# One program for ffn0's norm, scores, routing, placement and shared expert, with sixteen gathers issued at its end

## The reference, cut to what matters

```
def _L0_ffn_ref(x, w1s, w2s, w3s, W1, W2, W3, Wg):     # x is already normed
    def geglu(x, w1, w2, w3):
        return gelu(x @ w1) * (x @ w2) @ w3            # 128 -> 512 -> 128
    shared = geglu(xf, w1s, w2s, w3s)                  # every token
    idx = argmax(xf @ Wg, axis=-1)                     # one of 8 experts for a token
    final = sum over e of where(idx == e, geglu(xf, W1[e], W2[e], W3[e]), 0)
    return shared + final
x = x + 0.5 * _L0_ffn_ref(_layernorm(x), ...)
```

## Time and profile before

| | |
|---|---|
| three runs | 2185.0, 2183.94 and 2178.56 us; median 2183.94 |
| profiled execution, its own time | 2175.02 us |
| its span, first to last instruction | 2173.3 us |
| busy share of the span | PE 79%, PEld 65%, VectorE 64%, GpSimd 49%, ScalarE 38% |
| mean granted TensorE clock | 0.866 of full speed |

### The profile page before, as it was taken

One profiled execution on the slowest core, in us unless ns is written; L12 is line 12 of the kernel. 1 busy time (PEld: TensorE's weight loads), 2 busy tenths in 40 slices (PEclk: granted clock), 3 DMA queues, 4 the chain that ended last, 5 costly groups with the idle time before them and its releaser, 6 DMA issues. The chain is left out here.

```text
span 2173.3 us, 36779 instructions
## 1 busy us (share of the span) xinstructions
PE 1706.7 (79%) x11054; PEld 1406.2 (65%) x11054; DVE 1397.8 (64%) x3248; ACT 832.5 (38%) x1822; POOL 1068.3 (49%) x1178
## 2 busy tenths in 40 slices
PE   3889951499999999999976989547885488829883
PEld 3459950178888888888863579546874156628782
DVE  4444546499999999999854445484454544573455
ACT  1222212255555555555522222124552233225551
POOL 2006634267777777777630047436774100137772
PEclk9999965699999999999977999857998667659996
DMA  6001130000000000000022001231112100301114
GB/s 208 1 0 45 43 89 0 0 1 1 1 1 1 1 1 1 1 2 1 1 92 79 0 26 48 90 98 38 53 52 72 39 1 0 97 31 51 52 53 135
DMA packets 60900, 82.08 MB, mean 38 GB/s; under 512 B 24720, under 2 KB 30896, under 8 KB 60720
## 3 DMA queue, kind: packets, MB, share of 16 engines
q1 hardware_dynamic: 46640, 51.01, 7.5%
q0 software_dynamic: 14080, 28.86, 4.8%
HBM read 54.93 MB, written 24.90 MB: 37 GB/s over the span
## 5 line engine op out<-in xcount | busy, mean ns | idle before, releaser
L681 POOL DMA_INDIRECT rows_in<-xn_rows,slot_token x220 | 214.8, 976 | 334.6 <-SPq L676 268.8
L687 POOL DMA_INDIRECT y_rows<-y,slot_row x220 | 230.0, 1045 | 113.5 <-DVE y L814 53.4
L726 PE MATMUL ps<-w,inner_slot 128*128 x1760 | 246.3, 284 | 18.4 <-issue 7.7
L1466 DVE SCALAR_TENSOR_TENSOR cv<-ps,cw,cv 128x1021 f32<-128x1021 f32 (+2 forms) x192 | 245.0, 1276 | 17.3 <-ACT cv L1404 14.8
L714 PE MATMUL ps<-gT,w_slot 128*128 128x128 f32 x1760 | 242.1, 282 | 2.0 <-DVE hb L797 1.1
L726 PEld LDWEIGHTS ps<-w,inner_slot 128*128 128x128 f32 x1760 | 217.2, 194 | 30.8 <-issue 26.0
L714 PEld LDWEIGHTS ps<-gT,w_slot 128*128 128x128 f32 x1760 | 222.3, 198 | 4.5 <-issue 4.5
L1573 POOL TENSOR_TENSOR y<-t,sz 128x256 f32<-128x256 f32 x128 | 94.7, 740 | 181.4 <-DVE t L1510 181.4
L797 DVE TENSOR_TENSOR hb<-ps,b 128x512 f32<-128x512 f32 x142 | 97.6, 687 | 112.8 <-PE ps L714 81.6
L1311 PE MATMUL ps<-xnT,win 128*128 128x512 f32 x256 | 133.0, 645 | 31.8 <-DVE cv L1466 27.2
L252 PE MATMUL ps<-ident,xn 128*128 128x128 f32 x192 | 53.1, 432 | 118.7 <-DVE xn L212 118.7
(11 more groups left out here) (256 smaller groups left out, 4261.3 us busy)
## 6 DMA issues: line engine op xcount, KB each, us to landing
w<-in_L_ffn_W SPq DMA_DIRECT2D x6, 2048.0 KB, 11.3
back<-y_rows SPq DMA_DIRECT2D x48, 256.0 KB, 5.7
xn_rows<-xn SPq DMA_DIRECT2D x32, 256.0 KB, 3.9
rows_in<-xn_rows,slot_token POOLq DMA_INDIRECT x220, 2.6
y_rows<-y,slot_row POOLq DMA_INDIRECT x220, 2.3
out_x<-x SPq DMA_DIRECT2D x8, 256.0 KB, 3.5
win<-in_L_attn_in_w SPq DMA_DIRECT2D x1, 1544.0 KB, 10.4
b<-in_L_ffn_b SPq DMA_DIRECT2D x2, 512.0 KB, 11.2
```

The source lines that it names most:

```text
L681: nc.gpsimd.indirect_dma_start(k.rows_in[:, s % AHEAD, :], None, k.xn_rows[:, :], bass.IndirectOffsetOnAxis(ap=k.slot_token[:, s:s + 1], a ...
L687: nc.gpsimd.indirect_dma_start(kept, bass.IndirectOffsetOnAxis(ap=k.slot_row[:, s:s + 1], axis=0), k.y[:, s % RING, :], None).then_inc(sto ...
L726: ins = nc.tensor.matmul(py[:, s % DOWNS, :], k.inner_slot[:, s % RING, b * P:(b + 1) * P], w_dn[:, ds(e * (FB * D) + b * D, D)], start=(b ...
L1466: inc(V.scalar_tensor_tensor(out, piece[:, 0:SEQ - back], m.cw[:, c, i:i + 1], out, ALU.mult, ALU.add), tap_done if i < 2 else a["conv"])
```

## The change

ffn0's first three blocks become one, a new `shared`, and its program is written out for all 32 units with no loop. The norm of group `g + 1`, its transposes (`TURN`), scores (`SCORE`), the routing chain in five pieces, the counting matmuls (`COUNT`) and the placement (`PLACE`) stand between the units of the shared expert. The placement is done as in ffn1, with ScalarE's `match_lanes` and GpSimd's `match_tiles`. The transposes and the scores have one PSUM buffer each where they had two. The weights' semaphore is split: TensorE waits for the shared expert's three loads at its first unit, and SyncE waits for the rest at the end of the block. `rows_in` has 16 buffers, and GpSimd issues the gathers of slots 0 to 15 in this block, after `place_end`; `experts` begins with slot 16. `slot_expert` is written once. In ffn1's `route` the counting of the marks no longer waits for the Exp and the gates. Here is the core of the diff; `prepare` and `take_back` stay as they are, for the other stages.

```diff
+def match_lanes(k, act, n, slots, top):
+    r = n % 2
+    act.wait_ge(k.matched.sem, k.matched.at(n + 1))
+    act.wait_ge(k.placed.sem, k.placed.at(n - 1))
+    k.nc.scalar.activation(k.oh_slot[:, r, :, 0:slots], k.match[:, r, :, 0:slots], ACT.Copy,
+                           scale=k.lane[:, top - 1:top]).then_inc(k.lanes_put.sem, 1)
 def place_tensor(k, pe, n, slots):
     pe.wait_ge(k.onehot.sem, k.onehot.at(n + 1))
+    pe.wait_ge(k.lanes_put.sem, k.lanes_put.at(n + 1))
+    pe.wait_ge(k.tiles_put.sem, k.tiles_put.at(n + 1))
...
+def shared(k, shared_loads, expert_loads, slots, early):
+    TURN = {0: 1, 1: 2, 2: 3, 3: 4, 4: 5, 6: 6, 8: 7}
+    SCORE = {0: 0, 1: 1, 2: 2, 3: 3, 4: 4, 6: 5, 8: 6, 9: 7}
+    COUNT = 12
+    PLACE = {u: u - 17 for u in range(17, 25)}
...
+            statistics(0)                       # VectorE
+            statistics(1)
+            normalise(0)
+            for g in range(2, 5):
+                statistics(g)
+                normalise(g - 1)
+            for u in range(NU):
+                inner(u)
...
+                if u == 10:
+                    dve.wait_ge(logits_kept.sem, logits_kept.at(NG))
+                    route_choose(k, do, 0, L3)
+                if u == 11:
+                    marked(k, k.by_expert[0]).then_inc(marks.sem, 1)
+                if u == 13:
+                    dve.wait_ge(counted.sem, counted.at(1))
+                    route_ranks(k, do, ps_rank, ps_cnt)
+                if u == 14:
+                    route_bases(k, do)
+                if u == 15:
+                    route_positions(k, do, 1)
+                if 16 <= u < 24:
+                    match_vector(k, dve, u - 16, slots)
+                if u == 24:
+                    route_experts(k, do, slots)
+                if u == 25:
+                    place_end(k, dve, NG, slots, 1)
+                if u % FB == FB - 1 and u > FB:
+                    add(u // FB - 1)
...
+            for n in range(NG):                 # GpSimd, after the eight rstd
+                match_tiles(k, pool, n, slots)
+            pool.wait_ge(stored.sem, stored.at(NG))
+            pool.wait_ge(k.place_own.sem, k.place_own.at(5))
+            for s in range(early):
+                nc.gpsimd.indirect_dma_start(k.rows_in[:, s, :], None, k.xn_rows[:, :],
+                                             bass.IndirectOffsetOnAxis(ap=k.slot_token[:, s:s + 1], axis=0)
+                                             ).then_inc(gathered[s].sem, 16)
...
+            turn(0)                             # TensorE
+            for u in range(NU):
+                up_block(u)
+                if u in TURN:
+                    turn(TURN[u])
+                if u in SCORE:
+                    score(SCORE[u])
...
+                if u in PLACE:
+                    place_tensor(k, pe, PLACE[u], slots)
+                if u % FB == FB - 1 and u > FB:
+                    down_group(u // FB - 1)
+            down_group(NG - 1)
...
+            nc.scalar.activation(k.spare[:, 1:2], k.zero[:, 0:1], ACT.Gelu)   # ScalarE
+            copy(0)
+            for u in range(NU):
+                act.wait_ge(up.sem, up.at(u + 1))
+                act.wait_ge(ready.sem, ready.at(u - 1))
+                nc.scalar.activation(k.gl[:, u % 2, :], h1[:, u % 2, :], ACT.Gelu).then_inc(acted.sem, 1)
+                if u in TURN:
+                    copy(TURN[u])
+                if u in SCORE:
+                    keep(SCORE[u])
+                if 17 <= u < 25:
+                    match_lanes(k, act, u - 17, slots, 1)
...
 def experts(k, top, slots, early=0):
-    RING, AHEAD, LEADS = 4, 8, 13
+    RING, AHEAD, LEADS = 4, 16 if top == 1 else 8, 13
...
-                if t < slots:
+                if early <= t < slots:
                     gather(t)
...
-        prepare(k, k.wg0[:, :], NE, loads, True)
-        route(k, 1, SLOTS1, False)
-        shared(k, SLOTS1)
-        experts(k, 1, SLOTS1)
+        shared(k, shared_loads, expert_loads, SLOTS1, EARLY)
+        experts(k, 1, SLOTS1, EARLY)
```

More of the change, by code:

```diff
@@ new lines, in route_experts, with marked @@
+def route_experts(k, do, slots):
+    V = k.nc.vector
+    do(V.tensor_scalar(k.erow[:, 0:slots], k.iota[:, 0:slots], k.e8[:, 1, 1:2], None, ALU.is_ge))
+    for e in range(2, NE):
+        do(V.scalar_tensor_tensor(k.erow[:, 0:slots], k.iota[:, 0:slots], k.e8[:, 1, e:e + 1],
+                                  k.erow[:, 0:slots], ALU.is_ge, ALU.add))
+    do(V.tensor_copy(k.slot_expert[:, 0:slots], k.erow[:, 0:slots]))
+def marked(k, sel):
+    return k.nc.vector.tensor_copy(k.marks[:, :].rearrange("p (e t) -> p t e", e=NE), sel)
@@ L355, in route @@
+def route(k, slots):
     nc = k.nc
+    top, NB = 2, 2 * NG
     own = k.counter("route_vector_step")
@@ L385, in _ @@
[L385 to L397, removed]
@@ L407, in _ @@
[L407 to L415, removed]
@@ L416, in _ @@
[L416 to L424, removed]
@@ L425, in _ @@
-            for e in range(2, NE):
-                do(V.scalar_tensor_tensor(k.erow[:, 0:slots], k.iota[:, 0:slots], k.e8[:, 1, e:e + 1],
-                                          k.erow[:, 0:slots], ALU.is_ge, ALU.add))
-            for shift in range(4):
-                do(V.tensor_copy(k.slot_expert[:, shift, shift:shift + slots], k.erow[:, 0:slots]))
-            if alone:
-                place_end(k, dve, NB, slots, top)
+            route_choose(k, do, 0, L3)
+            do(V.scalar_tensor_tensor(r3[3], r3[0], -1e30, L3, ALU.mult, ALU.add))
@@ L432, in _ @@
+            do(V.tensor_mul(k.gate[:, 1, :], k.small[:, 0:NT], k.gate[:, 0, :]))
+            dve.wait_ge(counted.sem, counted.at(1))
+            route_ranks(k, do, ps_rank, ps_cnt)
+            route_bases(k, do)
+            route_positions(k, do, top)
+            for n in range(NB):
+                match_vector(k, dve, n, slots)
+            route_experts(k, do, slots)
+            place_end(k, dve, NB, slots, top)
             k.route_steps = do.n
@@ L561, in shared @@
     up, acted, ready, down_done, added = (k.counter(f"shared_{n}") for n in ("up", "acted", "inner_ready", "down", "added"))
+    gathered = [k.counter(f"slot_gathered{r}", 16, lead=0) for r in range(early)]
     w12, w3 = k.w12[:, NE, :], k.w3[:, NE]
     h1, h2, py = k.ps[:, 0:2, :], k.ps[:, 2:4, :], k.ps[:, 4:6, :]
-    NU = NG * FB
+    ps_s, ps_t = k.ps[:, 6, 0:GRP * NE], k.ps[:, 7, :]
+    ps_rank, ps_cnt = k.ps[:, 7, 0:NE * NT], k.ps[:, 7, NE * NT:2 * NE * NT]
+    L3 = k.logits[:, 0:NT * NE].rearrange("p (t e) -> p t e", e=NE)
@@ L630, in shared, with experts @@
+    shared_in.close(len(shared_loads))
+    expert_in.close(len(expert_loads))
+    for s in (var_ready, rstd_ready, xn_ready, own, pool_own, transposed, xt_copied, routed, logits_kept, stored):
+        s.close(NG)
     for s in (up, acted, ready):
         s.close(NU)
-    down_done.close(NG)
+    for s in (down_done, added):
+        s.close(NG)
+    route_own.close(k.route_steps)
+    marks.close(1)
+    counted.close(1)
     close_places(k, NG, 1)
-    added.close(NG)
-def experts(k, top, slots):
+def experts(k, top, slots, early=0):
@@ L665, in fetch @@
             _, held = nc.values_load_multi_w_load_instructions(
-                k.slot_expert[0:1, 0, first:first + count], engines=(engine,), min_val=0, max_val=NE - 1,
+                k.slot_expert[0:1, first:first + count], engines=(engine,), min_val=0, max_val=NE - 1,
                 skip_runtime_bounds_check_because="the table counts the experts whose first slot lies before a slot")
```

313 lines of the change are left out of this document (188 added, 125 removed).

## The result

The changed kernel takes 2116.81 us (median of 4 runs, 2112.67 to 2122.53) against 2181.25 for the kernel before (4 runs): ratio 0.971, 95% interval 0.9672 to 0.9748, faster by 64 us. The forecast was 2122.

A forecast was written before the change was run, and what follows sets the result against it. Before the experts, about 45 us with little TensorE work precede a TensorE-bound shared block. Gains of 35.3 + 33.0 - 2 x 5 + 3.2 = 61.5 us take 2175.0 to 2113.5, 2122 on the median; range 2108 to 2148.

The forecast's parts named there:

- TensorE's chain: Merged block of ffn0: TensorE works from the first xnT at 20.3 and ends at 127.9 us instead of 157.72.
- the 2.2 at the start: Start of TensorE's merged block: 2.2 us added for a clock that begins at 1.2 GHz instead of 2.4.
- the placements: Units 17 to 24: TensorE stops for the Gelu and match_lanes, 1.2 us eight times, 9.5 us a stage.
- The table load: ScalarE's Gelus in shared: one table load instead of one per group removes some 10 us of waiting a stage.
- VectorE's pieces at nothing: Merged block: VectorE's routing, match and one-hot pieces between inners cost nothing; uncovered, at most 10.5 us a stage.
- The entry: From ffn0's merged block to experts: GpSimd leaves last, at 130; first multiplication earlier by 35.3 - x and 33.0 - x us.
- x: GpSimd's DRAIN ahead of the barrier after sixteen gathers: taken as 5 us, bounds 0.03 and 6.43.
- 3.2 from the barrier: Start of experts: 3.2 us from the barrier to slot 0's first multiplication.
- The case of a long tail: Rival at the entry: sixteen back-to-back gathers leave a backlog, x is 20, time 2152 us; chance 0.12.
- Once running, `experts` is as before.: Expert passes of ffn0: fewer gathers left to GpSimd there save TensorE nothing.
- ffn1: ffn1's routing: waits for the Exp and the count cover each other, fewer slot_expert copies; 1.6 us, twice 3.2.
- The sum: Both ffn0 entries and ffn1 twice: 35.3 + 33.0 - 2 x 5 + 3.2 = 61.5 us gained.

The follow-up runs named there:

- Experiment 1: The changed kernel with each group's placement on TensorE one unit later (units 18 to 25 instead of 17 to 24); ratio 0.9601 to the kernel before.
- experiment 4: The kernel before with ScalarE's loop of the shared expert written out; ratio 0.9921 to the unedited kernel before.
- Experiment 11: The changed kernel with ffn1's routing in the order of before (Exp and gates ahead of the marks); ratio 0.9681 to the kernel before.

## Why the prediction was right

- *TensorE's chain.* Right, each term within 1.5 us: start 20.4 (forecast 20.3), TensorE busy for 99.6 us from there to its end (98.1 with the 2.2 at the start), idle for 8.4 at the placements (9.5), end 128.4 (127.9). `match_lanes` takes 0.42, not 0.35. Experiment 1 shows the term by taking it away. The 2.2 are there too: the first unit takes 3.54 us instead of 1.71 and the transposes behind it 0.85 instead of 0.44. That these ran at the lower level is read from the durations only; the granted clock of the profile reads 1.00 there.
- *The table load.* Right: 9.3 us in the first ffn0 by experiment 4 (148.4 against 157.7), 10 forecast.
- *VectorE's pieces at nothing.* Right: TensorE has no idle time between 22 and 74 us, in which the norms and the routing chain are made, nor between 106 and its end; in between it stops only at the placements, for ScalarE.
- *The entry.* The mechanism was right, GpSimd sets it, and two sizes were off. x was taken as 5 and is 2.2 and 2.4; 3.2 from the barrier was 2.5 and 1.5. Gains of 33.1 and 31.9 instead of 30.3 and 28.0. The 5 came from the DRAIN at the end of `experts`, and that one was indeed added time. It starts at 286.1 for 6.43 us, behind GpSimd's last scatter (timeline of before):

```profile
283.50 0.97 POOL L687 DMA_INDIRECT y_rows<-y,slot_row  x1 [0.30 <-issue]
```

What did not hold is to carry it over from a DRAIN behind scatters to one behind gathers. The case of a long tail took more gathers to mean a longer x as well; the DRAIN grew to 15.7, but the part behind the last gather did not.
- *"Once running, `experts` is as before."* Right on the first chip (124.1 and 122.9 us), wrong on the others, where the gathers ahead save 6.4 and 9.1 us in the two passes.
- *ffn1.* 1.6 forecast; to the first multiplication it is 1.58 (86.43 to 84.85 from the load back before it), and the stage as a whole 0.3 and 0.7. The difference lies in the passes, unedited, which took 190.0 and 188.0 us before and 191.3 and 189.3 after. Experiment 11 shows 1.2 of the 1.58.
- *The sum.* 61.5 forecast. The edited stages gave 68 in the profiled pair: 65 at the entries (58.3 forecast), 2 in ffn0's passes (nothing forecast) and 1 in ffn1 (3.2 forecast). The attention took 12 back, and the medians say 64. That 2122 lies so near 2116.8 is in part luck: the two entries were together 6.6 us better than forecast, and what the attention took back was in no term.
- *What it lacked* is a wait that no row of before named: instructions that come late while many indirect DMAs are issued. It costs nothing on the first chip. On the others it moves the first ffn0's last addition by 8.3 us and its first multiplication by 4.8, and the gathers' worth in the pass (6.4) makes up for that. That the ratio is 0.97 on both is in part this coincidence.

What makes the instructions late is not shown. That TensorE had them not yet, rather than waited for a semaphore, is inferred: the late matmuls have no wait in the program. The attention's 12 us stay open too: over the fourteen profiles of this study, with that stage the same in all, it takes from 196.0 (the kernel before) to 208.3 us (the change), and the kernel before alone had 196.0 and 205.0.

## What to carry to other kernels

A duration in an engine's queue (a DRAIN) counts from when the queue reached it, not from when the engine was free: price it by what lies between the end of the last work and its end, and from a place where the same kind of work stands ahead of it. When a copy is shared out to an engine, look at what stands ahead of it there; moving the consumer one unit later cost nothing and gave 10 us a stage, while moving the producer gave 5.7, since it brought up the next one. Work issued ahead of a barrier should be as much as the pass needs to start, not all that fits: on the chips of the experiments, with the stops gone, eight or twelve gathers ahead came to 0.954 of the time before, sixteen to 0.959 to 0.960. On the first chip this was not tried.

## What was not expected of the hardware

From the 13th of sixteen indirect DMAs issued at a pitch of 1.25 us, TensorE's instructions came one in 0.7 to 1.4 us until 2.9 us after the last, on three chips; with 5 or 8 of them nothing of TensorE's was late, with 12 it was 1.4 us. VectorE's addition (134.09 instead of 125.3) and ScalarE's Gelu (180.75, its matmuls done at 175.1) were late beside such gathers too. On the first chip fourteen delayed nothing. GpSimd's DRAIN after sixteen ended 2.2 us after the last gather's end, no longer than after eight (2.6), while behind the scatters of `experts` it ended 8 us after the last (284.5 to 292.5).
